# A gated cross-attention and expert block on one core: single-input SBUF instructions leave VectorE's loop, and both high-part casts go to ScalarE

## What is computed

```python
q = (layernorm(x) @ w_q);  k, v = split(context @ w_kv)
attn = softmax(q * SCALE @ k.T)
x = x + tanh(g_xattn) * tanh(gate) * ((attn @ v) @ w_out + b_out)
probs = softmax(layernorm(x) @ gate_w);  e = argmax(probs)
x = x + tanh(g_ffn) * prob_e * (relu(x_n @ w1[e]) @ w2[e])      # first 160 rows of each expert
```

## Time and profile before

| | us |
|---|---|
| median of 3 runs | 649.64 (649.15 to 649.65) |
| the profiled execution | 650.14 |
| its span in the trace | 648.4 |
| VectorE busy | 516.1 (80%) |
| TensorE busy | 471.8 (73%) |
| ScalarE busy | 349.8 (54%) |
| GpSimd busy | 324.8 (50%) |
| low-part subtractions on GpSimd (L506), 128 of them | 272.9 |

### The profile page before, as it was taken

The page is one execution under the profiler, slowest core; times in us unless marked ns, Lnnn a source line. Parts: engine busy times, 40 slices in busy tenths (PEclk is TensorE's granted clock), DMA queues, the critical chain, the costliest instruction groups (busy, mean ns, idle before and its releaser), DMA issues.

```text
span 648.4 us, 12904 instructions
## 1 busy us (share of the span) xinstructions
PE 471.8 (73%) x5068; PEld 379.6 (59%) x5068; DVE 516.1 (80%) x890; ACT 349.8 (54%) x547; POOL 324.8 (50%) x206
## 2 busy tenths in 40 slices
PE   6678769587796768677695777777596777856185
PEld 4356648465674657565584666656485556746184
DVE  4998997879888897879978898888978799886212
ACT  5656756555563665465464655635555566652031
POOL 3655555446454463545554374535644556644105
PEclk9799998788796997888897887968988889987578
DMA  7799999656765677648865776767757478766111
GB/s 202 208 180 163 188 221 178 122 107 121 133 130 106 102 146 143 124 82 147 146 100 105 118 125 135 122 104 119 142 104 139 79 122 139 142 121 132 25 67 41
DMA packets 285772, 83.14 MB, mean 128 GB/s; under 512 B 268403, under 2 KB 283171, under 8 KB 285712
## 3 DMA queue, kind: packets, MB, share of 16 engines
q1 hardware_dynamic: 284336, 79.01, 66.0%
q0 software_dynamic: 1376, 3.30, 1.4%
HBM read 10.83 MB, written 5.14 MB: 25 GB/s over the span
## 4 chain that ended last, share of the span: by engine, by line
PE 33%; DVE 30%; issue 19%; POOL 8%; ACT 7%; DMA 2%; POOLq 0%; SPq 0%; ACTq 0%
DVE MX L722 10%; POOL PARTS L506 7%; PE psEF L922 6%; PE psAB L997 4%; PE psEF L924 4%; DVE HL L709 4%; PE psEF L923 3%; PE psX L1083 3%; PE psCD L997 3%; ACT P L594 3%; DVE VL L715 3%; DVE NB L725 3%; ACT VH L567 2%; DVE winners L800 2%; PE psEF L1182 2%
## 5 line engine op out<-in xcount | busy, mean ns | idle before, releaser
L506 POOL TENSOR_TENSOR PARTS<-P,PARTS 128x1024 f16<-128x1024 f32 x128 | 272.9, 2140 | 261.5 <-DVE PARTS L734 212.1
L562 ACT ACTIVATE HL<-psEF 128x768 fp32r<-128x768 f32 x63 | 51.1, 811 | 161.3 <-PE psEF L924 161.3
L1019 PE MATMUL psO<-VH,PT 128*128 128x65 f16 x1024 | 114.7, 205 | 2.2 <-DVE O L747 1.7
L1020 PE MATMUL psO<-VL,PT 128*128 128x64 f16 x1024 | 114.4, 203 | 0.0
L1021 PE MATMUL psO<-VH,PT 128*128 128x65 f16 x1024 | 114.3, 204 | 0.0
L1019 PEld LDWEIGHTS psO<-VH,PT 128*128 128x128 f16 x1024 | 101.9, 105 | 3.4 <-DVE O L747 1.9
L1020 PEld LDWEIGHTS psO<-VL,PT 128*128 128x128 f16 x1024 | 101.9, 106 | 0.8
L1021 PEld LDWEIGHTS psO<-VH,PT 128*128 128x128 f16 x1024 | 101.9, 104 | 0.0
L594 ACT ACTIVATE P<-psAB,NB 128x512 f32<-128x512 f32 x128 | 80.9, 685 | 26.2 <-DVE NB L725 26.2
L594 ACT ACTIVATE P<-psCD,NB 128x512 f32<-128x512 f32 x128 | 81.4, 693 | 2.3
L922 PE MATMUL psEF<-cT_hi,w_hi 128*128 128x512 f32 x63 | 38.0, 604 | 60.6 <-issue 53.2
(11 more groups left out here) (172 smaller groups left out, 892.5 us busy)
## 6 DMA issues: line engine op xcount, KB each, us to landing
ctx_raw<-in_ctx_dram SPq DMA_DIRECT2D x8, 256.0 KB, 3.5
w1s<-in_L_ffn_w_dram SPq DMA_DIRECT2D x8, 256.0 KB, 3.3
PT<-PARTS SPq DMA_TRANSPOSE x128, 4.4
w2s<-in_L_ffn_w_dram SPq DMA_DIRECT2D x8, 256.0 KB, 4.6
experts_table<-zeros POOLq DMA_DIRECT2D x2, 645.0 KB, 4.2
PARTS<-experts_table SPq DMA_DIRECT2D x2, 516.0 KB, 4.2
wraw<-in_L_xattn_w_kv_dram SPq DMA_DIRECT2D x4, 256.0 KB, 5.5
out_dram<-row SPq DMA_DIRECT2D x8, 128.0 KB, 2.7
```

Of the source, the lines that this page charges most:

```text
L506: pool.tensor_tensor(PARTS[:, par, qt, 1], P32[:, par, qt], PARTS[:, par, qt, 0], ALU.subtract).then_inc(plo_done, 1)
L1019: pe.matmul(psO[:, g:g + DH + 1], phi, VH[:, kt, head, 0:DH + 1], start=first_, stop=False)
L1020: pe.matmul(psO[:, g:g + DH], phi, VL[:, kt, head, :], start=False, stop=False)
```

## The change

The scale of the scores is multiplied into `gamma` and `beta` (`norm_q`), so the exponential needs no scale and `NB` only adds a constant, as a tensor. Both casts of the probabilities are on ScalarE, the first between the two exponentials. `XN`, `xt_lo`, `tok` and both `vv` of the loop move to GpSimd (in the first and last batch's ends they stay). `xt_hi` moves from step 4 to the end of step 3, behind the second cast, and the transposition of `XN` to step 3. In the router, instructions with one SBUF input are replaced by instructions on two tensors; the counter `ROUTE` grows by one. The copy of the row ids goes to GpSimd. The diff, cut to its core:

```diff
+        norm_in = sb("norm_in", [P, 2], F32)
+        norm_q = sb("norm_q", [P, 2], F32)
+        lift2 = sb("lift2", [P, 2], F32)
...
-        X_STATS_STEP, XN_STEP, X_STEP = 0, 1, 4
+        X_STATS_STEP, XN_STEP, X_STEP = 0, 1, 3
...
             def x_rstd(b):
                 ts = slice(b * QT, b * QT + QT)
-                pool.wait_ge(xvv_done, b + 1)
+                if b == 0:
+                    pool.wait_ge(xvv_done, 1)
+                else:
+                    pool.wait_ge(xmv_done, b * QT + QT)
+                    pool.tensor_scalar(vv[:, ts], mv[:, ts, 1], 1.0 + EPS, EPS * EPS, ALU.mult, ALU.add).then_inc(xvv_done, 1)
+                    pool.wait_ge(xvv_done, b + 1)
                 pool.tensor_tensor(rstd[:, ts], vv[:, ts], mhalf[:, ts], ALU.pow).then_inc(xrstd_done, 1)
+
+            def xn(b):
+
+                pool.wait_ge(xrstd_done, b + 1)
+                pool.wait_ge(xt_psum, b)
+                for q, t in enumerate(x_tiles(b)):
+                    pool.tensor_scalar(XN[:, q, :], X1[:, t, :], mv[:, t, 0:1], rstd[:, t:t + 1], ALU.subtract,
+                                       ALU.mult).then_inc(xn_done, 1)
+
+            def xt_lo(b):
+                pool.wait_ge(xt_hi_done, b + 1)
+                pool.tensor_tensor(xT_lo[:, b % 2, :], XS[:], xT_hi[:, b % 2, :].bitcast(F32),
+                                   ALU.subtract).then_inc(xt_lo_done, 1)
...
+            def tokens(b):
+                pool.wait_ge(rstd_done, b + 1)
+                for q in range(QT):
+                    pool.tensor_scalar(tok[:, q, :], x_now[:, q, :], mv[:, q, 0:1], rstd[:, q:q + 1], ALU.subtract,
+                                       ALU.mult).then_inc(tok_done, 1)
...
-                pool.tensor_tensor(pool_mark[:], mhalf[:, 0:1], mhalf[:, 0:1], ALU.mult)
+                pool.tensor_copy(row[:, :, R_ID], ids[:, b * QT:b * QT + QT]).then_inc(id_done, 1)
+                pool.wait_ge(id_done, b + 1)
...
                         x_rstd(b + 1)
+                    if hp == XN_STEP and not is_last(b):
+                        xn(b + 1)
+                    if hp == X_STEP and not is_last(b):
+                        xt_lo(b + 1)
...
                         token_rstd(b - 1)
+                        tokens(b - 1)
...
-                                          ACT.Exp, bias=NB[:, par, qt, h:h + 1], scale=SCALE)
+                                          ACT.Exp, bias=NB[:, par, qt, h:h + 1])
...
-            def phi_second(b, hp):
+            def phi(b, hp, qt):
                 j = b * PAIRS + hp
-                act.wait_ge(exp_done, 2 * j + 2)
+                act.wait_ge(exp_done, 2 * j + qt + 1)
                 if j >= 2:
 
-                    act.wait_ge(pt_in[1][hp % 2], transposed_value(j - 2))
-                act.activation(PARTS[:, hp % 2, 1, 0], P32[:, hp % 2, 1], ACT.Copy).then_inc(phi_done[1], 1)
+                    act.wait_ge(pt_in[qt][hp % 2], transposed_value(j - 2))
+                act.activation(PARTS[:, hp % 2, qt, 0], P32[:, hp % 2, qt], ACT.Copy).then_inc(phi_done[qt], 1)
...
+            act.wait_ge(small_in, 32)
+            act.activation(norm_q[:], norm_in[:], ACT.Copy, scale=SCALE).then_inc(norm_scaled, 1)
+            act.wait_ge(norm_scaled, 1)
...
                     exps(b, hp, 0)
+                    phi(b, hp, 0)
                     exps(b, hp, 1)
                     if ot_group(b, hp):
                         ot_copy(*ot_group(b, hp))
-                    if hp == X_STEP and not is_last(b):
-                        xt_hi(b + 1)
...
-                    phi_second(b, hp)
+                    phi(b, hp, 1)
+                    if hp == X_STEP and not is_last(b):
+                        xt_hi(b + 1)
...
-                dve.tensor_scalar(NB[:, par, qt, :], MX[:, par, qt, :], SCALE, LIFT, ALU.mult, ALU.add)\
-                   .then_inc(bias_done, 1)
-
-            def phi_first(b, hp):
-                j = b * PAIRS + hp
-                dve.wait_ge(exp_done, 2 * j + 1)
-                if j >= 2:
-
-                    dve.wait_ge(pt_in[0][hp % 2], transposed_value(j - 2))
-                dve.tensor_copy(PARTS[:, hp % 2, 0, 0], P32[:, hp % 2, 0]).then_inc(phi_done[0], 1)
+                dve.tensor_tensor(NB[:, par, qt, :], MX[:, par, qt, :], lift2[:], ALU.add).then_inc(bias_done, 1)
...
-                dve.scalar_tensor_tensor(out=winners[:], in0=cand[:], scalar=0.0, in1=iota_e[:], op0=ALU.is_equal,
-                                         op1=ALU.mult).then_inc(route, 1)
+
+                dve.tensor_tensor(equal[:], lg, wide(lmax[:]), ALU.is_equal).then_inc(route, 1)
                 dve.wait_ge(route, n + 3)
+                dve.tensor_tensor(winners[:], equal[:], iota_e[:], ALU.mult).then_inc(route, 1)
...
-                dve.tensor_scalar(slotf[:], first[:], float(CAP), float(E * CAP - 1), ALU.mult, ALU.add).then_inc(route, 1)
-                dve.wait_ge(route, n + 9)
+                dve.tensor_tensor(slotf[:], first[:], cap1[:].to_broadcast([P, QT]), ALU.mult).then_inc(route, 1)
+                dve.wait_ge(route, n + 10)
...
-                    phi_first(b, hp)
...
-                    if hp == XN_STEP and not is_last(b):
-                        xn(b + 1)
-                    if hp == X_STEP and not is_last(b):
-                        xt_lo(b + 1)
...
-                    if hp == TOK_STEP and not is_first(b):
-                        tokens(b - 1)
```

More of the change, by code:

```diff
@@ L80, in gated_block @@
         ident = sb("ident", [P, P], F32)
-        gamma = sb("gamma", [P, 1], F32)
-        beta = sb("beta", [P, 1], F32)
+        norm_in = sb("norm_in", [P, 2], F32)
+        norm_q = sb("norm_q", [P, 2], F32)
+        lift2 = sb("lift2", [P, 2], F32)
+        cap1 = sb("cap1", [P, 1], F32)
+        last1 = sb("last1", [P, 1], F32)
+        dropped1 = sb("dropped1", [P, 1], F32)
         gates = sb("gates", [P, 3], F32)
@@ L145, in gated_block @@
         slotf = sb("slotf", [P, QT], F32)
+        posf = sb("posf", [P, QT], F32)
+        equal = sb("equal", [P, QT, E], F32)
         over = sb("over", [P, QT], F32)
@@ L183, in gated_block @@
         small_in = sem("small_in")
+        norm_scaled = sem("norm_scaled")
         w_in = [sem(f"w_in{i}") for i in range(6)]
@@ L247, in gated_block @@
         slot_done = sem("slot_done")
+        id_done = sem("id_done")
         scattered = sem("scattered")
@@ L345, in gated_block @@
         psEF2 = psEF[:].rearrange("p (i n) -> p i n", i=2)
-        MOMENTS_STEP, TOK_STEP, TOKT_STEP, LOGITS_STEP, RANKS_STEP = 4, 5, 5, 6, 7
+        MOMENTS_STEP, TOKT_STEP, LOGITS_STEP, RANKS_STEP = 4, 5, 6, 7
         BO_STEP, BIAS_STEP = 2, 2
-        ROUTE = 16
+        ROUTE = 17
+        FULL = float(E * CAP - 1)
         OUT_GROUPS = ST_TILES // 2
@@ L463, in _ @@
             pool.memset(hot_padded[:], 0.0).then_inc(pool_consts, 1)
-            pool.memset(taken[:], 0.0).then_inc(pool_consts, 1)
+            pool.memset(taken[:], FULL).then_inc(pool_consts, 1)
+            pool.memset(cap1[:], float(CAP)).then_inc(pool_consts, 1)
+            pool.memset(last1[:], FULL + CAP).then_inc(pool_consts, 1)
+            pool.memset(dropped1[:], DROPPED).then_inc(pool_consts, 1)
             pool.iota(ids[:], pattern=[[P, TT]], base=1, channel_multiplier=1,
@@ L479, in token_rstd @@
             def token_rstd(b):
-                pool.wait_ge(vv_done, b + 1)
-                pool.tensor_tensor(rstd[:, 0:QT], vv[:, 0:QT], mhalf[:, 0:QT], ALU.pow).then_inc(rstd_done, 1)
+                if is_last(b):
+                    pool.wait_ge(vv_done, b + 1)
+                else:
+                    pool.wait_ge(mv_done, b * QT + QT)
+                    pool.tensor_scalar(vv[:, 0:QT], mv[:, 0:QT, 1], EPS, None, ALU.add).then_inc(vv_done, 1)
+                    pool.wait_ge(vv_done, b + 1)
+                pool.tensor_tensor(rstd[:, 0:QT], vv[:, 0:QT], mhalf[:, 0:QT], ALU.pow).then_inc(rstd_done, 1)
+            def tokens(b):
[3 more added lines that the diff above has]
+                                       ALU.mult).then_inc(tok_done, 1)
             def scatter(b):
@@ L544, in xt_hi @@
                 act.wait_ge(xt_psum, b + 1)
-                if b == 0:
-                    act.wait_ge(small_in, 32)
-                else:
+                if b:
                     act.wait_ge(xt_lo_done, b)
-                act.activation(XS[:], x_bank(b)[:, 0:SQ], ACT.Identity, bias=beta[:, 0:1],
-                               scale=gamma[:, 0:1]).then_inc(xt_f32, 1)
+                act.activation(XS[:], x_bank(b)[:, 0:SQ], ACT.Identity, bias=norm_q[:, 1:2],
+                               scale=norm_q[:, 0:1]).then_inc(xt_f32, 1)
                 act.wait_ge(xt_f32, b + 1)
@@ L675, in x_moments @@
                 ts = slice(b * QT, b * QT + QT)
-                dve.tensor_scalar(vv[:, ts], mv[:, ts, 1], 1.0 + EPS, EPS * EPS, ALU.mult, ALU.add)\
-                   .then_inc(xvv_done, 1)
+                if b == 0:
```

(6 more changed lines are left out.)

40 lines of the change are left out of this document (21 added, 19 removed).

## The result

The changed kernel takes 610.99 us (median of 4 runs, 610.42 to 611.46) beside 649.39 us of the kernel before (4 runs, 649.12 to 649.65): ratio 0.9408, 95% interval 0.9392 to 0.9425. The forecast was 595, range 578 to 620. The profiled execution took 610.42 us, of which the span is 608.7; the span before was 648.4, so 39.7 us went.

What follows compares the result with a forecast made beforehand. Bound: the loop NB, VectorE's cast, two GpSimd subtractions, with VectorE's SBUF instructions stalled behind GpSimd. Gains 52.6 + 1.3 + 2.2 - 1.2 = 54.9 us off 650.14 gave 595.2, less 0.5: about 595, range 578 to 620.

Steps and rivals of the forecast that it cites:

- Does tensor by tensor escape the stall?: VectorE's NB, winners, slotf with two SBUF inputs: claimed to wait for GpSimd's subtraction just the same, no gain.
- Rival A: Tensor-by-tensor instructions on VectorE do escape the stall: 61 us a batch, about 556 us; chance 5 in 100.
- The new loop through ScalarE: Casts on ScalarE delay GpSimd's subtractions: short step 7.74 us with an extra copy, 7.24 without, instead of 7.14.
- That is a loss where no other stall stood: Short steps get slower through ScalarE's casts, from 7.14 to 7.74 or 7.24 us: steps 0 and most of batch 0.
- GpSimd's one-input price: A 128x128 one-input instruction on GpSimd taken at 0.45 us; tok ends 2.0 us after N, a step's first NB end.
- rival C: GpSimd's one-input instruction very slow: gain gone at 3.2 us each, about 670 us at 4; chance 3 in 100.
- Steps 5, 6 and 1: Steps of a middle batch: 7.55 us with a 256-element copy, 9.5 with winners stalled, 7.75 with a copy on ScalarE.
- The ends: Batch 0 gains 1.3 us, its bo step taking 8.7; batch 7 gains 2.2; tail and start cost 1.2.
- rival B: GpSimd instructions cost 1 us or more, second NB waits, or steps 0.3 us later: 605 to 625 us; 20 in 100.
- The likeliest case: The forecast itself for the whole kernel: 595 us, own range 583 to 605, chance 69 in 100.

Runs made afterwards that it cites:

- experiment 1: Changed kernel with NB computed again by the tensor_scalar form with one SBUF input: 611.71 us, ratio 0.9391.
- experiment 2: Changed kernel with XN, tok and both vv back on VectorE, casts and xt_lo staying as changed: 632.41 us, ratio 0.9741.
- experiment 3: Kernel before the change with only the casts on ScalarE, the first between the exponentials: 634.70 us, ratio 0.9789.
- experiment 4: Changed kernel with the first cast back on VectorE behind kq_lo, the moves staying: 586.87 us, ratio 0.9048.
- experiment 8: Changed kernel with one more unused 128x128 GpSimd instruction ahead of the two XN of each batch: 611.97 us.
- experiment 9: Changed kernel with tok's transposition and ScalarE's copy of it put behind v_project and v_hi in step 5: 603.25 us, ratio 0.9278.
- experiments 5 and 6: Changed kernel with NB made by a TENSOR_REDUCE over two elements: 603.51 us; the same with the first cast also back on VectorE: 577.43 us.

## Why the prediction was right, and where it was off

**Does tensor by tensor escape the stall? Right.** It doesn't: `NB`, `winners` and `slotf` still end with a subtraction, as `rank_hot` in the earlier trace rows said, and experiment 1 finds no time in it for `NB`. For the router it was not tried alone. Experiments 2 and 3 differ in it, among other things, and in batch 4 steps 6 and 7 are no shorter with it (10.85 and 9.59 us) than without (10.53 and 9.23). Rival A (556 us) is out. The rule of the Trainium skill, SBUF — State Buffer, section "Who interferes with whom", that two SBUF inputs contend with GpSimd's reads, agrees with 1.18 and 1.30 us for the `NB` of step 2 beside the subtraction. Beside GpSimd's `XN`, which reads SBUF too, it does not: the second `NB` of that step took 0.16 us, and the measurement decides.

**The new loop through ScalarE. Right.** 7.75 forecast, 7.70 or 7.71 measured in steps 0 and 2, with the casts within 0.05 us of their places. Step 3 came at 8.51 (8.6), 4 at 8.17 (8.05), 7 at 9.10 (9.25).

**"That is a loss where no other stall stood". Right as put, incomplete in what it suggests.** Step 0 grew by 0.56 us, as said. The forecast priced casts and moves in one sum and never asked what the casts bring to the kernel before. They open pauses between the subtractions, worth 19.2 us there (experiment 3). The sum wasn't harmed by that, because with the moves in place those stalls are gone either way, as experiment 4 shows. But the other half of the sentence is where the change leaves time behind: with the cast left on VectorE the kernel is 24 us faster (experiment 4).

**GpSimd's one-input price: mis-sized.** 0.45 us taken between 0.30 and 0.73; 0.79 and 0.80 measured, above both ends. For `XN` nothing follows from it (experiment 8). For `tok` it does: I had it end at N + 2.0, at most + 2.4; it ended at + 2.80 (325.33 + 1.59 against 324.12), after the moment from which `v_project` could run, which experiment 9 shows at N + 2.25 (257.98 against 255.73). A smaller part of that lateness is the start: `tok` began at N + 1.21, where rival C's sum has 0.95. (With that 0.95 and 0.45 for each `tok` the end is 1.85 rather than 2.0, and rival C's batch at d = 4 is 3.4 us worse rather than 3.6. Neither changes the forecast.)

**Steps 5, 6 and 1: the term that made most of the miss.** Forecast 7.55, 9.5 and 7.75; measured 8.08, 10.46 and 8.26 in batch 4, together 2.0 us of the batch, and 1.85 on average over batches 1 to 6, of 1.9 that each misses. The late `tok` made step 5 long (experiment 9: 7.49 without it). Of step 6 I had priced `winners` right, 2.06 us, but had its exponential start at N; at the lower clock `kq_hi` comes 1 us later, and where the clock stays up the step is 9.45, the forecast's 9.5 (in batch 2 of the changed kernel, whose step 5 has 1.00, and in three batches of experiment 9). Of the clock the forecast said only that it would be nearer 1.00 in steps 2 and 5; it is 1.00 in step 2 (0.74 before) and 0.79 in step 5 (0.67 before). Step 1's excess goes with the same delay of `kq_hi` behind step 0. In batches 1 and 2 step 0 has the clock at 1.00 and step 1 takes 7.71 and 7.70 us, the forecast's 7.75; in batches 3 to 6 the clock is 0.78 and step 1 takes 8.26 to 8.29. The stretch of step 0 of batch 2, after; that of batch 4 is the first of the table above:

```profile
149.48:157.18 7.70, 4.83 (x49) 3.70 (x50) 6.33 (x13) 6.21 (x9) 6.21 (x4) 1.00 0.65 136
```

The two go together in all six batches; no run changed the clock alone, and what lowers it stays open.

**The ends.** Batch 0 gave 0.3 us instead of 1.3, batch 7 1.6 instead of 2.2. In batch 0 the 8.7 us that I had put on the step of `bo` were not there: `bo` took 0.29 us (2.13 before) and its step 7.20. But steps 1, 3 and 4 took 8.64, 8.31 and 8.18, where I had 7.24 or 7.75; why was not looked into. The tail costs 3.3, where its terms came to 0.9: there I had counted no stall of `over` and `slot_now`, and no clock. They took 2.10 and 2.00 us, and the last but one output projection ran at half clock. The two tensor inputs are not what stalls `over`: in experiment 3, where it has one input as before, it took 2.06 us. It is now issued just after a subtraction has begun. From the tail's timeline after:

```profile
545.26 2.10 DVE L866 TENSOR_TENSOR over<-pos,last 128x2 f32<-128x2 f32 x1
```

The stretch of that projection, after:

```profile
550.50:556.00 5.50, 5.46 (x28) 5.43 (x29) 0.00 (x0) 0.00 (x0) 2.08 (x2) 0.50 0.65 119
```

With `XN`, `tok` and `vv` back on VectorE (experiment 2) the tail is 63.5 us, just the 0.9 more that I had counted, and with the casts alone (experiment 3) it is 63.5 too, though `over` and `slot_now` are stalled in both: so these hide beside the last pair. In the kernel of experiment 2 the second half of the projection, twelve matmuls, took 1.62 us where it takes 2.77 here. That is half of the missing 2.4; the other half, and why the clock stayed low, are not settled.

**The account.** Forecast gain 54.9 us of the profiled execution, measured 39.7. Missing in batches 1 to 6 are 11.5 (52.6 less 41.1), in batch 0 1.0, in batch 7 0.6, in the tail and the start 2.1: 15.2 in all. That is what rival B described, in size and in part in mechanism (GpSimd's one-input instructions near 0.8 us); two of its conditions, 1 us for such an instruction or a second `NB` waiting behind it, did not come about, and its third, each step 0.3 us late, only as a sum: 11.1 of the 15.2 us stand in steps 5, 6 and 1 of batches 1 to 6, while steps 2, 3 and 7 came as forecast. The likeliest case's own range, 583 to 605, did not hold the time; the wider one, which took in B, did. So the mechanism of the gain was right and the time lay in the range by the room left for B, not by the sum.

## What to carry to other kernels

Ask of each moved piece what is queued behind its consumer: `XN` and `tok` cost the same on GpSimd, and 0.8 us a batch more ahead of the one was free, while the same ahead of the other cost 3.8 us in all. And when a change has several parts, price each both alone and with the rest: the casts gained 19 us without the moves and cost 22 with them. A wait that only an instruction's form causes may go with another form: a reduction over two elements did what neither the one-input nor the two-input addition could. And when one wait is gone, look at what was counted from its end: `tok` was at N + 2.80, and with the earlier N of experiments 5 and 6 at N + 3.86 and N + 4.24; putting it behind `v_project` gave 7.7 us in the first case and 14 in the last.
